# Routed tiles in the order of steps, block 0's norm inside them, and a reordered opening of attention 2

## The reference, cut to what matters

```
x = x + cross_attention_0(layernorm(x), ctx)      # 16 heads, 77 keys
x = x + ffn_0(layernorm(x))                       # this change: its second half
x = x + cross_attention_1(layernorm(x), ctx, ctx) # "attention 2": this change: its opening
x = x + fp8_linear(layernorm(x))

ffn_0(x): scores = softmax(x @ gate.T); the 2 best of 8 experts per token, weights = their scores
          z = sum over the 2 of weight * (y * silu(g)) @ W2[e].T, (y, g) = split(x @ W1[e].T)
          z = z + shared gated MLP(x)

cross_attention_1(q, k, v): Qp = q @ Wq + bq; Q = l2norm(Qp); K = l2norm(k @ Wk + bk); V = v @ Wv + bv
          softmax per head, out @ Wo + bo + Qp, layernorm * gamma + beta
```

## Time and profile before

| | us |
|---|---|
| median of 3 runs | 994.44 (992.12 to 996.5) |
| profiled execution | 993.44 |
| its span | 991.7 |
| PE busy in the span | 905.3 (91%) |
| DVE busy | 777.0 (78%) |
| ACT busy | 541.8 (55%) |
| POOL busy | 354.5 (36%) |

### The profile page before, as it was taken

The page is one execution under the profiler, slowest core; times in us unless marked ns, Lnnn a source line. Parts: engine busy times, 40 slices in busy tenths (PEclk is TensorE's granted clock), DMA queues, the critical chain, the costliest instruction groups (busy, mean ns, idle before and its releaser), DMA issues. The chain is left out here.

```text
span 991.7 us, 17877 instructions
## 1 busy us (share of the span) xinstructions
PE 905.3 (91%) x5517; PEld 760.3 (77%) x5517; DVE 777.0 (78%) x1843; ACT 541.8 (55%) x1477; POOL 354.5 (36%) x409
## 2 busy tenths in 40 slices
PE   6899999999999999999899999748999999999635
PEld 6899999999999989898799999746655555554324
DVE  7789788788789788887577777766578888867988
ACT  5667577567567555452344444424555655554277
POOL 3243334334334256675400000077446455311330
PEclk9999999999999999999899999966999999999758
DMA  9899950000000033341233334351111011000004
GB/s 309 292 321 319 316 182 0 0 0 1 31 0 2 1 102 128 112 139 64 81 123 123 125 123 123 96 142 49 53 33 38 17 43 43 1 1 0 1 2 168
DMA packets 52760, 91.84 MB, mean 93 GB/s; under 512 B 5351, under 2 KB 27600, under 8 KB 52688
## 3 DMA queue, kind: packets, MB, share of 16 engines
q1 hardware_dynamic: 46544, 74.16, 24.0%
q0 software_dynamic: 6144, 16.79, 5.2%
HBM read 34.56 MB, written 56.36 MB: 92 GB/s over the span
## 5 line engine op out<-in xcount | busy, mean ns | idle before, releaser
L500 POOL TENSOR_TENSOR prob<-prob,row_inv 128x462 f32<-128x462 f32 (+1 forms) x96 | 83.7, 874 | 180.3 <-DVE row_inv L676 180.2
L863 PE MATMUL acc<-u,probT 128*128 128x256 f32 (+1 forms) x960 | 134.0, 288 | 0.9 <-DVE u L688 0.9
L2337 POOL DMA_INDIRECT routed<-dispatched,slots x64 | 65.8, 1028 | 176.4 <-POOLq L1464 158.9
L560 ACT ACTIVATE prob<-score,neg_max 128x77 f32<-128x77 f32 x512 | 120.8, 350 | 14.5 <-DVE neg_max L670 14.3
L816 PE MATMUL score<-m,xnT 128*128 128x462 f32 (+1 forms) x576 | 124.4, 354 | 0.0
L863 PEld LDWEIGHTS acc<-u,probT 128*128 128x128 f32 (+1 forms) x960 | 119.3, 189 | 1.8 <-DVE u L688 1.3
L816 PEld LDWEIGHTS score<-m,xnT 128*128 128x128 f32 x576 | 97.6, 191 | 6.1
L550 ACT ACTIVATE probT<-tr 128x512 fp32r<-128x512 f32 (+1 forms) x96 | 51.9, 543 | 66.3 <-PE tr L802 66.0
L1439 POOL DMA_INDIRECT dispatched<-xn,slots x64 | 69.5, 1087 | 44.7 <-DVEq L1302 27.5
L1893 PE MATMUL score<-qT,kbd 128*128 128x512 f32 (+1 forms) x240 | 79.5, 442 | 0.9 <-DVE qT L2118 0.7
L665 DVE TENSOR_TENSOR probT<-tr,probT 128x512 fp32r<-128x512 f32 (+1 forms) x96 | 56.6, 592 | 12.8 <-ACT probT L550 12.4
(11 more groups left out here) (386 smaller groups left out, 2242.9 us busy)
## 6 DMA issues: line engine op xcount, KB each, us to landing
dispatched<-zeros SPq DMA_DIRECT2D x1, 33664.0 KB, 113.1
xn<-dispatched SPq DMA_DIRECT2D x71, 128.0 KB, 2.0
dispatched<-hid SPq DMA_DIRECT2D x71, 128.0 KB, 1.7
out<-x_res SPq DMA_DIRECT2D x7, 512.0 KB, 2.6
x_res<-in_x SPq DMA_DIRECT2D x1, 3072.0 KB, 16.7
consts<-in_L_ffn_W SPq DMA_DIRECT2D x8, 384.0 KB, 3.5
consts<-in_L_ffn_Ws SPq DMA_DIRECT2D x3, 384.0 KB, 4.4
x_res<-in_x SPq DMA_DIRECT2D x2, 512.0 KB, 9.2
```

The costliest lines, as they stand in the source:

```text
L500: gp.tensor_tensor(pr, pr, row_inv[t % 2][:, heads(k)].unsqueeze(2).to_broadcast([P, BANK_HEADS[k], KEYS]), ALU.mult).then_inc(prob_ready, 1)
L560: last = act.activation(prob[t % 2][:, h * KEYS:(h + 1) * KEYS], score_of(t, k)[:, n * KEYS:(n + 1) * KEYS], ACT.Exp, bias=neg_max[t % 2][ ...
L863: last = pe.matmul(acc[t % 2][:, 0:D], probT[t % 2][i][0:rows, c, :], u[k][0:rows, c, :], start=(c == 0 and q == 0), stop=(c == KCH - 1 an ...
L2337: gp.indirect_dma_start(out=routed[n % 2][:, k, j, :], out_offset=None, in_=xd, in_offset=bass.IndirectOffsetOnAxis(ap=g["slots"][:, n, k, ...
```

## The change

It has four parts.

1. **Order of the tiles.** A tile is now a pair (step, expert): step k of an expert is rows 128k to 128k + 127 of its region. Tiles run through all experts' step 0, then step 1, and so on. After 32 tiles every routed row of block 0 is stored, after 64 every one of block 1 (`FIRST_TILES`). The lists come from 128 partitions, one for each pair: constants are made on POOL and DVE during the shared MLP (`dve_pairs`, 13 DVE instructions in block 1), three DVE instructions compare them with the counts (`dve_used`), and nine small matmuls (`pe_places`, `pe_lists`) with six DVE operations turn them into places. `dve_list` is gone.
2. **Inside the tiles.** After store 4, SP issues the 7 loads of attention 2's context and weights (`next_loads`). The maximum and exponential for `share` move ahead of the tiles (one more table switch on ACT on each side), and the rest of `share` is spread over iterations 6 to 11 on DVE. POOL waits for the first 32 stores, gathers block 0's rows, scales and adds them itself (four operations on 128x1024), and computes 1/std; DVE's norm statistics stand in iterations 50 to 54, the shift at 57, ACT's `xn` at 60 to 63. POOL then waits for 64 stores and issues block 1's 8 gathers, and only then reaches the barrier. SP no longer waits for the last stores at the barrier, but for the 7 loads.
3. **Attention 2's opening.** Block 0's loads, gathers, combine, statistics and xn are gone from it. DVE combines block 1 there. PE's order is now context, transposes of xn, keys, queries, values. POOL does `kbd` for both halves before block 1's 1/std, and then block 2's gathers, after waiting for all stores.
4. **Memory.** `routed`, the first three blocks of `xf` and the norm buffers lie where the shared MLP's tiles were (allocated from the right side), so that they exist during the routed tiles.

The diff, cut to its core:

```diff
 def pe_block(pe, n):
+                if n == LAST and c == 0:
+                    pe_places(pe)
+                if n == LAST and c == 1:
+                    pe_lists(pe)
 # SP, routed tiles
                 for i in range(TILES_B):
                     if i + XT_BUFS - 2 < TILES_B:
                         load(i + XT_BUFS - 2)
+                    if i == TILES_B - 1:
+                        sp.wait_ge(s["xT_mm"], TILES_B)
+                        sp.sem_clear(range(xt_in[0].num, xt_in[-1].num + 1))
                     store(i)
-                for k in range(YT_BUFS):
-                    sp.wait_ge(stored[k], 16 * len(range(k, TILES_B, YT_BUFS)))
+                    if i == 4:
+                        next_loads()
+                sp.wait_ge(s["next_in"], 16 * NEXT_LOADS)
 # POOL, end of the stage
+        def gp_next_block(gp):
+            gp.wait_ge(s["down_mm"], SH_USES)
+            gp_stored(gp, FIRST_TILES[0])
...
+            for k in range(TOP_K):
+                part, share = g["routed"][0][:, k, :, :], g["share"][:, 0, k, :].unsqueeze(2).to_broadcast([P, TJ, D])
+                gp.tensor_tensor(part, part, share, ALU.mult).then_inc(s["x_scaled"], 1)
...
+                gp.tensor_tensor(g["x"][:, 0, :, :], g["x"][:, 0, :, :], part, ALU.add).then_inc(s["x_added"], 1)
+            gp.wait_ge(s["x_mv"], 1)
+            inverse_std(gp, g, g["rstd3"], g["mean_var3"][:, :, 1], s["x_eps"], 1, s["x_rstd"])
+            gp_stored(gp, FIRST_TILES[1])
...
 # POOL, shared MLP: constants of the pairs, behind scatter 0
+                gp.iota(tile_i[:, :], [[1, TILES_B + 1]], 0, 0).then_inc(s["filled"], 1)
...
 # DVE, routed tiles
-                    if i == TILES_B - 3:
-                        dve_route_shift(dve)
+                    if i >= WEIGHTS_AT:
+                        dve_route_weights(dve, i - WEIGHTS_AT)
+                    if i >= NEXT_NORM:
+                        dve_next_norm(dve, i - NEXT_NORM)
                 dve_tile_out(dve, TILES_B - 1)
-                dve_route_weights(dve)
 # POOL, attention 2's opening
-                gp_gather(gp, 0)
                 gp.memset(vb[:, :, :, :, :], 0.0).then_inc(s["vb_zero"], 1)
-                gp_gather(gp, 1, 0, 4)
-                gp_ln(gp, 0)
                 gp.wait_ge(s["norm_out"], 1)
                 gp.tensor_tensor(knorm[:, :], knorm[:, :], g["half"][0:KEYS, 0:B], ALU.pow).then_inc(s["norm_pow"], 1)
-                gp_gather(gp, 1, 4)
-                gp_keys(gp, 0, 0)
                 gp_root(gp, 0)
-                gp_keys(gp, 0, 1)
-                gp_gather(gp, 2, 0, 2)
+                for f in range(DC):
+                    gp_keys(gp, 0, f)
                 gp_ln(gp, 1)
-                gp_gather(gp, 2, 2)
+                for k in range(YT_BUFS):
+                    gp.wait_ge(g["stored"][k], 16 * len(range(k, TILES_B, YT_BUFS)))
+                gp_gather(gp, 2)
```

More of the change, by code:

```diff
@@ L970 @@
 REST = H2 - P
+STEPS = P // E
+LIST_COLS = 3
 REGION = T
@@ L976 @@
 TILE_LEAD = 3
+WEIGHTS_AT, NEXT_NORM, NEXT_SHIFT, NEXT_X = 6, 50, 57, 60
+FIRST_TILES = [E * TB * (n + 1) // P for n in range(2)]
 STAGES = 2
@@ L987, in experts @@
         ws1, gate = g["ws1"], g["gate"]
-        ws2 = [sb(f"ws2T{i}", [P, SHARED, D], F32R) for i in range(2)]
+        ws2 = g["ws2"]
         w1 = [sb(f"w1T{i}", [P, DC, E, UP], F32R) for i in range(2)]
@@ new lines, in dve_next_norm @@
+        def dve_next_norm(dve, i):
+            stats, mean_var = g["stats3"], g["mean_var3"]
+            if i == 0:
+                dve.wait_ge(s["x_added"], TOP_K)
+            if i < TJ:
+                dve.bn_stats(stats[:, i, :], x_tile(0)(i))
+            if i == TJ:
+                dve.drain()
+                for j in range(TJ):
+                    last = dve.bn_aggr(mean_var[:, j, :], stats[:, j, :])
+                last.then_inc(s["x_mv"], 1)
+            if i == NEXT_SHIFT - NEXT_NORM:
+                dve.wait_ge(s["x_rstd"], 1)
+                dve.scalar_tensor_tensor(g["shift3"][:, :], mean_var[:, :, 0], -1.0, g["rstd3"][:, :], ALU.mult, ALU.mult).then_inc(s["x_shift"], 1)
@@ L1569, in _ @@
                         act_tile_silu(act, i + 2)
[L1570 to L1571 removed]
+                    if i - NEXT_X in range(TJ):
+                        act_next_norm(act, i - NEXT_X)
             @block.vector
@@ L1681, in attention1 @@
         y = sb("y3", [P, TJ, D], F32)
-        routed = [sb(f"routed{i}", [P, TOP_K, TJ, D], F32) for i in range(2)]
+        routed = g["routed"]
         score = [pb(f"score3_{s}") for s in range(2)]
@@ L2003, in act_last_norm @@
             for j in (2 * a, 2 * a + 1):
-                last = act.activation(g["xf"][:, n, j, :], x_tile(n)(j), ACT.Identity, scale=f_rstd[:, j:j + 1], bias=f_shift[:, j:j + 1])
+                last = act.activation(g["xf"](n)[:, j, :], x_tile(n)(j), ACT.Identity, scale=f_rstd[:, j:j + 1], bias=f_shift[:, j:j + 1])
             if a == 1 or n == LAST:
@@ L2180, in dve_divide @@
                 dve.wait_ge(s["proj_mm"], proj_count(n - 1, 1, 1))
+            elif i == 0:
+                for m in range(YT_BUFS):
+                    dve.wait_ge(g["stored"][m], 16 * len(range(m, TILES_B, YT_BUFS)))
             if i < DC:
@@ L2333, in gp_gather @@
         def gp_gather(gp, n, first=0, last=TOP_K * TJ):
-            if n >= 2 and first == 0:
-                gp.wait_ge(s["both_added"], n - 1)
+            if n >= 3 and first == 0:
+                gp.wait_ge(s["both_added"], n - 2)
             for k, j in (divmod(i, TJ) for i in range(first, last)):
@@ L2752, in program @@
         g["kT"] = g["consts"][:, :].rearrange("p (a c) -> p a c", a=PAIRS)
+        g["stored"] = [ctx.enter_context(nc.semaphore(f"stored1_{i}")) for i in range(YT_BUFS)]
+        g["gathered1"] = [ctx.enter_context(nc.semaphore(f"gathered1_{k}")) for k in range(TOP_K)]
         with ExitStack() as stages01:
-            opening_buffers(nc, g, stages01)
+            shared = ExitStack()
+            opening_buffers(nc, g, stages01, shared)
             with ExitStack() as weights0:
```

363 lines of the change are left out of this document (220 added, 143 removed).

## The result

The changed kernel took 1008.52 us, the median of 4 runs (1002.67 to 1014.52), beside 995.31 for the kernel before (992.12 to 996.5, 4 runs). The ratio is 1.0129, 95% interval 1.0072 to 1.0186: slower by 13 us. The forecast was 987, faster. The profiled execution is the longest of the four, 1014.52 us, with a span of 1012.8: 21.1 more than before's 991.7.

A forecast was written before the change was run, and what follows sets the result against it. PE bounds the tiles; the change attacks 44 us of short steps between last store and first score, with no engine full. Terms -14.3 + 5.0 + 1.5 + 0.2 + 1.0 = -6.6 from 993.44 gave 987 us, range 979 to 995.

The forecast's parts named there:

- opening: Attention 2's start: first score moves from 684.55 to 670.2, a gain of 14.3 us, bounds 11.2 and 15.3.
- seven loads, tile 11: SP's queue in the tiles: seven issues delay load 11, whose margin is 0.4 us; cost 5.0, bounds 0 and about 8.
- block 0's gathers: In the tiles: they share DMA engines with tile loads and lengthen landings; cost 1.5 us, bounds 0 and 5.5.
- block 1's gathers: End of the tiles: they come after the last load and cost nothing.
- rest of the tiles: DVE's added weights and statistics lie in its idle time in the tiles; cost 0.2 us, up to 1.
- shared MLP and lists: Small DVE and POOL instructions in the shared MLP's first blocks cost 1.0 us (0 to 2); the old list's 5 return nothing.
- It arrives with SP, give or take 1 us: Barrier before attention 2: POOL, after 8 gathers taking 10.1 us, gets there when SP does, within 1 us.
- wait of DVE's shift for POOL's 1/std: Attention 2's opening: DVE's shift of block 1 waits several us for POOL, ended by 1/std at 666.9.
- the 0.6 for queuing behind them: In the tiles: load 11 queuing behind the seven transfers adds 0.6 us to PE's stop, making 3.8.
- the 1.2 for the clock: In the tiles after PE's stop: half clock would cost 2.5 us; half of that, 1.2, was taken.
- The rival "slower": Tile loads from rows 4096 apart land at 2.6 instead of 2.0 us, costing 13 us: 1000; chance 0.10.
- POOL's arithmetic beside the tiles' DVE work: In the tiles: POOL's four operations of about 2.39 us each cost nothing; if they excluded DVE, 8 us.

The follow-up runs named there:

- e1: The changed kernel again with no edit, on chip B: 998.45 us against 991.78 for the kernel before, ratio 1.0071.
- e15: e13's kernel with block 0's gathers behind 40 stores instead of 32 and its norm six iterations later, chip E: 988.18 us, ratio 0.9953.
- e13: e8's kernel again, as base on chip E: 989.95 us, ratio 0.9959.
- e16: e8's kernel with block 0's gathers one in two tiles, its norm later, and the seven loads spread over every second store, chip E: 983.27 us, ratio 0.9885.
- e3: The changed kernel with the 16 gathers of blocks 0 and 1 replaced by zero-filling memsets, chip B: 987.84 us, ratio 0.9953.
- e6: The changed kernel with waits for block 1's gathers to land and a marking memset at POOL's end of the tiles, chip C: 1012.33 us, ratio 1.0160.
- e5: The changed kernel with block 1's gathers moved from POOL's end of the tiles to its start of attention 2, chip C: 1007.75 us, ratio 1.0123.
- e7: The kernel before with a look-ahead of 8 tile loads instead of 6, chip C: 989.92 us, ratio 0.9943.
- e2: The changed kernel with SP's look-ahead in the tiles at 8 loads instead of 6, chip B: 982.07 us, ratio 0.9903.
- e17: e16's kernel again with more rounds, chip F: 975.78 us, ratio 0.9832.
- e8: The changed kernel with both look-ahead 8 and block 1's gathers in the opening, chip C: 994.29 us, ratio 0.9979.
- e9: e8's kernel again, as base on chip D: 979.08 us, ratio 0.9873.
- e4: The changed kernel with POOL's constants for attention 2 held back until the lists are ready, chip B: 999.47 us, ratio 1.0069.

## Why the prediction was wrong

By its own terms, in us. The column B is e1's span against before's (994.8 and 991.7), A the first profile's. Gaps are counted over 2.07.

| term | forecast | B | A |
|---|---|---|---|
| opening | -14.3 | -6.6 | -13.5 |
| seven loads, tile 11 | +5.0 | +7.6 | +7.6 |
| block 0's gathers | +1.5 | +0.7 | +6.9 |
| block 1's gathers | 0 | +0.4 | +6.7 |
| rest of the tiles | +0.2 | +0.3 | +2.4 |
| shared MLP and lists | +1.0 | +1.5 | +5.8 |
| ahead of the shared MLP | 0 | +0.9 | +4.4 |
| first load to first copy | 0 | -1.4 | +1.0 |
| behind the first score | 0 | -0.4 | -0.2 |
| sum | -6.6 | +3.0 | +21.1 |

The medians say +6.7 on B and +13.2 on A; one profile is one execution, the one on A is the slowest of its four, and before's is not from chip B. So the sums are good for which term moved, not for the last us.

Two steps failed, and which of them sets the time depends on the chip.

- **The step that failed in the first result** is the pair of terms for the gathers in the tiles: 1.5 for block 0's, because they would lengthen the landing of tile loads, and "Block 1's gathers come after the last load and cost nothing". They cost 6.9 and 6.7, the largest miss of column A. PE waited for no tile's load beside block 0's row there. ACT and DVE stood still instead, with their inputs ready, and PE waited behind them, so a gather after the last load costs as much as one before it. On A, C and E a dense row does this in the tiles; on B, D and F it costs next to nothing (0.7 and 0.4 in e1). e15 against e13 shows that the stall goes with the gathers, and e16 that it is gone with a wide spacing. (The kernel without gathers, e3, ran only on B, so no run takes a stall away by taking the gathers away.) What it is that the engines lack then is open: not an input, and not a place in ACT's list of instructions.
- **The step that failed on every chip** is "It arrives with SP, give or take 1 us", of POOL at the barrier. The arrival of the gathers was right to 1 us: they ended 0.97 after SP's last store was issued (650.74 and 651.71 in e1). But a stage that POOL ends with gathers opens 6.86 us later. e6 shows that it isn't their landing, e3 and e5 that it goes when they aren't the end. In the kernel before nothing shows it, since POOL's scatters end 165 us ahead of the barrier. I had bounded every unknown cost but this one; "POOL must reach the barrier too" asked for a bound. In the first result it cost almost nothing, because the late tiles covered it: that column A's opening, -13.5, is so near to my -14.3 is luck.
- **The rest of column A.** The 5.8 of the shared MLP and the lists hold DVE's "remote" waits beside the scatters, which the kernel before has as well in e7, and one `at_place` of 3.68 that no other profile has. The 4.4 ahead of the shared MLP are chance. I had put nothing on any of these waits.
- **The opening behind the barrier was right**, in time and in mechanism. I had 29.3 us from start to first score (640.9 to 670.2); it is 29.5 in e1 (658.5 to 688.04). The wait of DVE's shift for POOL's 1/std is there with 5.20. POOL's power took 2.40 instead of 1.04 beside DVE's combine, but it ended while DVE was at the query biases, and the keys' projection had a mean granted clock of 0.87, so that its 24 matmuls took 3.46 us for my 3.1.
- **The seven loads** cost 7.6 and not 5.0, near my upper bound of 8. The issues were right (3.5 us later). Two sizes were wrong: the 0.6 for queuing behind them was 2.0 or more in e1 and e2, and the 1.2 for the clock was about 2.4, the 7.6 less PE's wait of 5.21. The clock fell as feared: 0.50 in 510 to 514 us of e1, 0.83 in the 4 us behind.
- **The rival "slower"**, landings at 2.6 us by the new order of tiles, didn't come: the median landing stayed 2.0. Slower came true by other mechanisms.
- **POOL's arithmetic beside the tiles' DVE work** cost nothing, as forecast: in e17 the four operations run there and no gap exceeds 2.3.

## What to carry to other kernels

The end of a stage can cost more on one engine than on another: before work is moved to the end of an engine's list, look in the trace for a stage that ended that way, and where there is none, bound the barrier like any other unknown. A reserve of 0.4 us on the loads of the engine that bounds is worth mending before anything is put on its queue; here two buffers that lay idle gave 6 us to the kernel before and 16 to the changed one. And run a change on more than one chip: the same kernel (e8, e9, e13) stood at 0.987 on one and 0.996 to 0.998 on two others, and in the first profile the gathers in the tiles cost 14 us that cost 1 in e1.

## What the runs showed of the hardware that I had not expected

- From POOL's last instruction to the next stage it is 6.85 to 6.86 us if gathers stand at the end of its list, landed or not (the first profile, e1, e2, e4, e6).
- Chips differ in what a dense row of indirect DMAs does to other engines: in the tiles ACT was idle for up to 5.4 us (e5), ended by a "remote" event, on A, C and E, never on B, D and F. The kernel before, too, is 2 to 4 us slower on C and E than on B, D and F (995.6 and 994.3 against 991.8, 992.1 and 992.0).
- A load of 128 KB behind seven transfers of 1.25 MB together was taken up 3.5 us (e5) to 6.05 us (e9) after its issue, with PE waiting for it each time, instead of landing after the usual 2.0.
